# Rows of products moved from SBUF to SBUF, one transfer per sequence, instead of through memory in groups of four tiles

## What is computed

```python
x_norm = _rmsnorm(x, norm_weight)
k = _phi(jnp.einsum('btd,fd->btf', x_norm, Wk))
v = jnp.einsum('btd,ed->bte', x_norm, Wv)
def step(M, kv):                       # 64 steps, one per token
    k_t, v_t = kv
    v_pred = jnp.einsum('bf,bfd->bd', k_t, M)
    surprise = jnp.linalg.norm(v_t - v_pred, axis=-1, keepdims=True)
    M = M + eta_c[None, :, None] * surprise[:, :, None] * (k_t[:, :, None] * v_t[:, None, :])
    return (_ln2(M), None)
```

## Time and profile before

| | us |
|---|---|
| median of 3 runs (1952.49 to 1954.5) | 1952.64 |
| the profiled execution, its own time | 1955.59 |
| its span, first to last instruction | 1953.9 |
| busy in the span: PE | 1311.3 |
| DVE | 1370.8 |
| ACT | 1133.0 |
| POOL | 1030.3 |
| DMA packets | 192277, 148.11 MB |

### The profile page before, as it was taken

How to read it: one execution, slowest core, us unless ns; L and a number is a source line. 1 busy time by engine, 2 the same in 40 slices (tenths; PEclk the granted TensorE clock), 3 DMA queues, 4 the chain that set the end, 5 groups by cost and what they waited for, 6 DMA issues and landing times. The chain is left out here.

```text
span 1953.9 us, 60466 instructions
## 1 busy us (share of the span) xinstructions
PE 1311.3 (67%) x18195; PEld 1070.9 (55%) x18196; DVE 1370.8 (70%) x4870; ACT 1133.0 (58%) x3308; POOL 1030.3 (53%) x1566
## 2 busy tenths in 40 slices
PE   6999995888858729996654999100000786849990
PEld 5777773666646618995653677100000565639990
DVE  5999994877787754453555666499999577755574
ACT  4777772777746616774554555365556565626674
POOL 3666664455559967777862444011111453867663
PEclk9999996999989969997886999655555898969995
DMA  3333331311112213333443454200000422323343
GB/s 88 98 94 97 97 98 41 112 49 49 51 45 72 69 44 91 97 97 116 135 136 93 89 109 83 41 1 1 1 1 5 153 67 62 86 59 90 88 114 115
DMA packets 192277, 148.11 MB, mean 76 GB/s; under 512 B 19458, under 2 KB 179586, under 8 KB 191746
## 3 DMA queue, kind: packets, MB, share of 16 engines
q1 hardware_dynamic: 178818, 118.93, 23.2%
q0 software_dynamic: 13312, 27.49, 4.3%
HBM read 76.54 MB, written 61.34 MB: 71 GB/s over the span
## 5 line engine op out<-in xcount | busy, mean ns | idle before, releaser
L1035 PE MATMUL ffn_run_up_ps<-ffn_run_xt,ffn_run_w_now 128*128 128x128 f32 x1792 | 250.5, 284 | 47.3 <-DVE ffn_run_h L1163 19.9
L1005 POOL DMA_INDIRECT expert_outputs<-ffn_run_y_all,ffn_run_ids x224 | 219.0, 978 | 87.6 <-issue 45.2
L1035 PEld LDWEIGHTS ffn_run_up_ps<-ffn_run_xt,ffn_run_w_now 128*128 128x128 f32 x1792 | 225.8, 198 | 59.1 <-ACT ffn_run_xt L1071 30.2
L778 POOL DMA_INDIRECT tokens_by_expert<-ffn_x_all,ffn_dest x192 | 192.8, 1004 | 52.6 <-issue 45.5
L1779 PE MATMUL mixer_m_ps<-mixer_mine,mem_state_coef 128*64 128x64 f32 x4 | 0.5, 334 | 284.2 <-DVE mixer_off_in L1913 284.2
L1044 PE MATMUL ffn_run_y_ps<-ffn_weights,ffn_run_h 128*128 x1216 | 174.0, 277 | 0.7 <-DVE ffn_run_y_all L1180 0.5
L1511 POOL TENSOR_TENSOR recur_rho<-recur_var_eps_new,k_pack 128x1 f32<-128x1 f32 x64 | 34.9, 545 | 248.4 <-DVE recur_var_eps_new L1605 248.4
L1779 PEld LDWEIGHTS mixer_m_ps<-mixer_mine,mem_state_coef 128*64 128x64 f32 x4 | 0.3, 206 | 284.3 <-DVE mixer_ones L1911 284.3
L1044 PEld LDWEIGHTS ffn_run_y_ps<-ffn_weights,ffn_run_h 128*128 128x128 f32 x1216 | 155.5, 194 | 1.1 <-issue 1.1
L1072 ACT COPY ffn_run_w_now<-ffn_weights 128x512 f32 x224 | 139.4, 622 | 0.1
L382 POOL TENSOR_TENSOR self_k_ex<-self_kt,k_pack 128x256 f32<-128x256 f32 x128 | 75.9, 614 | 116.7 <-ACT self_kt L569 116.7
(11 more groups left out here) (335 smaller groups left out, 4697.6 us busy)
## 6 DMA issues: line engine op xcount, KB each, us to landing
ffn_run_x<-tokens_by_expert SPq DMA_DIRECT2D x56, 260.0 KB, 2.9
tokens_by_expert<-fill_zeros SPq DMA_DIRECT2D x32, 292.5 KB, 2.8
ffn_run_yg<-expert_outputs SPq DMA_DIRECT2D x16, 512.0 KB, 4.7
memory_rows<-products_row SPq DMA_DIRECT2D x16, 390.0 KB, 4.6
ffn_weights<-memory_rows SPq DMA_DIRECT2D x16, 390.0 KB
tokens_by_expert<-fill_zeros SPq DMA_DIRECT2D x32, 162.5 KB, 2.6
ffn_weights<-in_pack_ffn SPq DMA_DIRECT2D x1, 4112.0 KB, 14.8
self_turned<-in_x_turned SPq DMA_DIRECT2D x64, 64.0 KB, 1.8
```

Source lines behind the costliest of these rows:

```text
L778: pool.indirect_dma_start(xs[h], bass.IndirectOffsetOnAxis(ap=self.dest[:, r, t:t + 1], axis=0), self.x_all[:, t, :], None)\
L1005: pool.indirect_dma_start(ys, bass.IndirectOffsetOnAxis(ap=ids[:, t:t + 1], axis=0), y_all[:, t, :], None)\
L1035: mm = nc.tensor.matmul(up_ps[t.slot(2)][:, c * P:(c + 1) * P], w_now[:, t.slot(2), c * P:(c + 1) * P], xt[:, t.slot(2), :], start=True, s ...
```

## The change

The tensor in memory and both transfers through it go. In their place SP issues two transfers for each tile as soon as its rows are there, one per sequence: 64 partitions of 780 bytes in `row` to one partition of `room`. The rest of SP's step keeps its order: the load of x, with its wait, comes behind the stores of its step. DVE's wait for a free slot counts the eight transfers of a group (`(uses - 1) * 128`). SP's last waits are for the stores alone.

```diff
-        rows_v = rows_out.rearrange("(g n p) r -> g p n r", p=P, n=4)
-        batch_v = rows_out.rearrange("(g b t) r -> g b (t r)", b=8, t=S)
-        rows_back = sem("rows_back")
...
                 t = i + -1
-                if t.exists() and t.c % 4 == 3:
+                if t.exists():
                     n, slot, uses = four(t)
                     sp.wait_ge(row_ready, t.count())
                     sp.wait_ge(row_copied, t.count())
-                    sp.dma_start(rows_v[n], row[:, slot, :, :]).then_inc(stored[slot], 16)
-                t = i + -5
-                if t.exists() and t.c % 4 == 3:
-                    n, slot, uses = four(t)
-                    sp.wait_ge(stored[slot], uses * 16)
-                    sp.dma_start(room[bass.ds(n * 8, 8), 0:S * ROW], batch_v[n]).then_inc(rows_back, 16)
+                    for b in range(2):
+                        sp.dma_start(room[2 * t.n + b:2 * t.n + b + 1, 0:S * ROW],
+                                     row[b * S:(b + 1) * S, slot, t.c % 4, :]).then_inc(stored[slot], 16)
                 t = i + 11
                 if t.exists() and t.c % 4 == 0:
...
-            for c in range(-11, NT + 5):
+            for c in range(-11, NT + 1):
                 step(kind(0, c))
             for s in stored:
-                sp.wait_ge(s, 16 * NT // 8)
-            sp.wait_ge(rows_back, 16 * NT // 4)
+                sp.wait_ge(s, 32 * NT // 2)
...
                     if t.c % 4 == 0 and t.after(8):
-                        dve.wait_ge(stored[slot], (uses - 1) * 16)
+                        dve.wait_ge(stored[slot], (uses - 1) * 128)
```

More of the change, by code:

```diff
@@ L1216, with memory_products @@
 N_MEM = float(F * D)
-def memory_products(nc, stage, k, x_in, w_all, w_norm, eta, rows_out, room, k_all, v_all, qt_all, eta_col):
+def memory_products(nc, stage, k, x_in, w_all, w_norm, eta, room, k_all, v_all, qt_all, eta_col):
     with ExitStack() as ctx:
@@ L2004, in build @@
             run_experts(nc, f, k, xs[0], ys[0], x1)
-        rows = nc.dram_tensor("memory_rows", (B * S, ROW), F32, kind="Internal").ap()
         with ExitStack() as ffn_ctx:
@@ L2011, in build @@
                 k_all, v_all, qt_all = mm.sb("k_all", [P, NT, F]), mm.sb("v_all", [P, NT, D]), mm.sb("qt_all", [P, NT, P])
-                memory_products(nc, "products", k, x1, part["w_all"], part["w_norm"], part["eta"], rows, f.weights, k_all, v_all, qt_all, eta[:, :])
+                memory_products(nc, "products", k, x1, part["w_all"], part["w_norm"], part["eta"], f.weights, k_all, v_all, qt_all, eta[:, :])
                 memory_recurrence(nc, "recur", k, f.weights, coef, offset[:, :])
```

## The result

The changed kernel takes 1987.69 us (median of 4 runs, 1985.35 to 1990.78) against 1952.57 us (4 runs, 1951.83 to 1954.5): a ratio of 1.0179, 95% interval 1.0161 to 1.0198, +35.1 us. The forecast was 2025.0 us, +72.7: the direction and the mechanism came out, the size is half. A second measurement of the same kernel (`after_again`) gave 1989.01 us against 1955.12, ratio 1.0169 (1.0136 to 1.0203).

A forecast was written before the change was run, and what follows sets the result against it. PE bounds the products stage before, the stores' destination after: first packet at 1072.6, 63 tiles x 3.90 = 245.7 us, plus 4.24, so the recurrence starts at 1322.6 instead of 1249.84. 1952.64 + 72.7 = 2025 us, range 1980 to 2072.

The forecast's parts named there:

- What bounds, what can be won and lost: Products stage: PE sets the pace; at most the 20.09 us gap can be won, the cover in 168 us lost.
- issue times: On SP: 128 transfers instead of 32, 0.9 us of issue per 2.66 us tile period, hidden.
- the backlog never runs dry: SP's stores: four tiles (15.6 us) are queued when the wait is released, the next issued after 8 to 11 us.
- The price of a tile: Stores into `room`: 99,840 bytes into two neighbouring partitions at 25.6 GB/s, 3.90 us a tile, above PE's 2.66.
- one at a time: Stores into `room`: a tile's bytes move into its two neighbouring partitions one after the other, 3.90 us a tile.
- The loads of x, 0 to 12 us: Queue shared with the stores: loads of x fit beside held-up transfers, 0 us, or 12 us at the upper end.
- VectorE's wait and the clock: Products stage: DVE waits some 60 us for stores in 14 or so waits; transfers stay the bound if the clock varies.
- The gap: Between last row and recurrence: no shorter than before, some 20 to 35 us, with five to eight tiles still queued.
- the branch that was forecast: Products stage bound by the destination of the stores: 1997 to 2069 us, chance 0.76.
- in series: Rival for the stores: each transfer pays 1.6 us to landing without overlap, 3.2 us a tile, 1981 us; chance 0.04.
- the faster one: Rival: 51.2 GB/s, 1.95 us a tile, PE stays the bound, 12.9 us earlier, 1939.7 us; chance 0.13.
- Far worse: Rival: engines at one partition disturb each other, 14.4 GB/s, 6.9 us a tile, 2217 us; chance 0.05.

The follow-up runs named there:

- after: The changed kernel itself, two transfers per tile straight into `room`, against the kernel before: 1987.7 us, ratio 1.0179.
- xnone: Changed kernel without loads of x from the third group on, products made from old x: 2003.8 us, ratio to the kernel before 1.0256.
- crowd_xnone: Changed kernel, eight transfers in a row to partitions c to c+3 and c+32 to c+35, no loads of x from the third group on: 2015.9 us.
- deep: Changed kernel with `row` holding 16 tiles instead of 8, exponentials written over their input: 1973.7 us, measured again (deep_again) 1969.2; median of all ten runs 1970.9.
- xnone_free: Changed kernel without loads of x from the third group on and without SP's wait in front of their place: 1994.1 us, ratio 1.0206.
- spread: Changed kernel with eight transfers in a row going to eight places at least four partitions apart: 1943.7 us, ratio 0.9939.

## Why the prediction was right in direction and wrong in size

- **What bounds, what can be won and lost:** right. The gap fell by 5.8 us and the cover before it was lost, 32.7 us; nothing after it moved.
- **SP:** issue times were hidden as said. "From then on there is always a backlog" and "the backlog never runs dry" were wrong. The prediction had itself put down that SP holds tiles 1 to 3 of each group behind x; the queue of a bunch, four tiles at 3.2 us instead of 3.9, lasts 12.8 us instead of 15.6, and the next one came 10.8 to 16.6 us after it instead of 8 to 11, so that it was sometimes empty first. It was never asked at which price that turns. Windows after and `xnone` show the idle engines; taking the hold away is worth 9.7 us where no x is loaded.
- **The price of a tile, the term that was mis-sized:** 3.90 us was taken; in the prediction's own frame it is (1279.7 - 4.2 - 1075.8) / 63 = 3.17 us, with the first packet at 1074.81 (the first bunch of stores) + 0.95. 63 x 0.73 = 46 us, less the 3.1 us by which that bunch left later, is the whole error of 43 us in the recurrence's start. The 25.6 GB/s itself is right, as the plateau of 24 to 28 in `xnone` shows; `crowd_xnone`, with four tiles in a row to one place and no x, comes nearest to the forecast's tile, at 3.77 us. The step that failed is "one at a time": transfers follow each other without a pause, an engine that has finished its pieces goes on to the next transfer, and after every second tile that is another place (`crowd_xnone` has half as many such seams as `xnone`, 3.77 us against 3.51). This gives 30 GB/s (3.33 us) while stores are queued; with the loads of x it is 3.17 to 3.30 in after.
- **The loads of x, 0 to 12 us:** wrong in sign. They save some 15 us here, 0 with the place spread, and 12.7 in the deep kernel.
- **VectorE's wait and the clock:** the mechanism is right, the wait is half (29.2 of some 60 us), by the same mis-sized price. The clock does fall to 0.50 behind the long waits and is 0.93 over the stage. That the transfers stay the bound when the clock goes up and down does not hold everywhere: in `xnone_free` they are idle most of 1160 to 1180, at a clock of 0.74. `deep`, with no wait for a store in its profiles, goes from 1988 to 1970.9, 17 of the 35 us; since its queue does not run dry either, that is more than waits and clock alone. The other half stays even when VectorE doesn't wait: in the profile of `deep` the start of the recurrence is 5.7 us later than before, in that of `deep_again` 8.2, and the median of the ten is 16 us above before. What the slower ones among them lose has no profile.
- **The gap:** forecast as 20 to 35 us with five to eight tiles queued, measured 14.3, of which SP waits 10.5 us for the last stores, some three tiles at 3.2 us. With 16 tiles of room it is 18.7 and 14.9.
- **The range:** the branch that was forecast, a stage bound by the destination, was given 1997 to 2069 and missed. That 1987.7 lies in the stated range of 1980 to 2072 is luck: the range reaches so low for the "in series" rival alone.
- **The rivals:** the faster one (36.4 GB/s as the point where the sign turns) lost, but `deep` runs at 37 and misses by little; the "in series" rival stood at 1981, close to the result, and its reason does not hold: in `spread` the same transfers, each with its own latency, keep up at 2.68 us a tile. "Far worse" lost: two partitions do take what one takes.

## What to carry to other kernels

Ask of a transfer not only how many bytes and engines it has but which partitions it and its neighbours in the queue write: small transfers into neighbouring partitions, one after the other, share one limit of about 26 GB/s (`crowd_xnone`). Moving every other one 64 partitions away (`halves`, 1942.7 us) turned +35 us into -12, and setting the rows of one transfer four apart (`back_spread`, 1944.3) cut the old path's gap from 20.1 to 11.3 us. A price per transfer that is right alone is not the rate of a queue: look for what the engines do at the seams between transfers. And where a wait stands in front of a transfer in an issuer's program, work out whether the queue behind it runs dry before the next bunch is issued.

## What the runs showed of the hardware that was not expected

- One load of eight rows of 49,920 bytes takes 6.9 us a packet into eight neighbouring partitions and 2.46 us into partitions four apart.
- Two places served at the same time take about twice as much as one: in `halves`, with two places 64 partitions apart, the stores run at 50 to 70 GB/s behind the loads of x, against 24 to 28 into one place in `xnone`, and keep up with PE at a DMA share of 0.50. The Trainium skill, in SBUF — State Buffer, section "Can I just issue two DMAs to hit both halves?", says that two transfers at once, to partitions 0 and 64, were only 6% faster than one; `halves` against after (0.9932 against 1.0179 of before) speaks against taking that as a rule for a queue of small ones.
- Transfers that share the queue can speed up those that a place limits: 256 KB loads of x over all partitions save some 15 us, 64 KB over all partitions or cuts to 8 partitions save nothing.
- The 16 parts of one transfer may end up to 7.8 us apart (after_again; 7.7 in after and `deep`).
